# Expert slots of two widths in a routed transformer block: 64 of 256 rows and 7 of 128, written out

## What is computed

```
x = x + attention_block(layernorm(x))        # linear attention, 16 heads, MLP of 1024
xf = layernorm(x)
logits = xf @ gate_w.T                       # 8 experts
the 2 largest per token, softmax over the 2  # comb[token, expert]
out = sum over e of comb[:, e] * ((silu(xf @ wg[e].T) * (xf @ wu[e].T)) @ w_down[e].T)
shared = silu(xf @ sg_gate.T) * (xf @ sg_up.T) @ sg_down.T
x = x + shared + out
```

## Time and profile before

| | |
|---|---|
| median of 3 runs | 1746.89 us (1745.64 to 1747.42) |
| profiled execution, its own time | 1744.85 us |
| its span, first to last instruction | 1742.7 us (2.15 us lie around it) |
| PE / DVE / POOL / ACT busy | 96% / 67% / 67% / 52% of the span |
| mean granted clock of PE | 0.985 |
| first phase / expert phase | to about 1142 us / from there on |

### The profile page before, as it was taken

The page is one execution under the profiler, slowest core; times in us unless marked ns, Lnnn a source line. Parts: engine busy times, 40 slices in busy tenths (PEclk is TensorE's granted clock), DMA queues, the critical chain, the costliest instruction groups (busy, mean ns, idle before and its releaser), DMA issues.

```text
span 1742.7 us, 25628 instructions
## 1 busy us (share of the span) xinstructions
PE 1680.7 (96%) x7243; PEld 1227.5 (70%) x7289; DVE 1166.9 (67%) x1968; ACT 904.1 (52%) x2240; POOL 1166.9 (67%) x624
## 2 busy tenths in 40 slices
PE   6899999999999999999999998989999999999997
PEld 4555666666666666666666665578888888888886
DVE  7989999999999999999999993322222222222221
ACT  4356667667667667667667646522322322332322
POOL 5769889889889889889889881413333343343343
PEclk9898999999999999999999999999999999999999
DMA  4302211211211211111111111367777777777764
GB/s 151 116 13 61 62 49 37 62 49 36 61 49 36 61 49 36 59 50 36 54 55 37 37 49 37 92 169 162 165 154 160 165 157 156 167 158 156 168 158 78
DMA packets 89455, 157.20 MB, mean 90 GB/s; under 512 B 8896, under 2 KB 72128, under 8 KB 89024
## 3 DMA queue, kind: packets, MB, share of 16 engines
q1 hardware_dynamic: 60512, 112.58, 20.9%
q0 software_dynamic: 28896, 44.06, 14.9%
HBM read 101.79 MB, written 48.56 MB: 86 GB/s over the span
## 4 chain that ended last, share of the span: by engine, by line
PE 89%; ACT 5%; DVE 2%; issue 2%; DMA 1%; POOL 1%; SPq 1%; POOLq 0%; ACTq 0%; DVEq 0%
PE p_b L1494 17%; PE p_b L1548 13%; PE p_b L1698 10%; PE p_b L1709 10%; PE p_b L1641 8%; PE p_q L1698 7%; PE p_q L1466 6%; PE p_v L1698 4%; PE p_v L1466 3%; PE p_b L1480 2%; PE p_xT L1685 2%; PE p_xT L1626 2%; ACT rows L706 1%; ACT xmid L706 1%; PE p_b L1588 1%
## 5 line engine op out<-in xcount | busy, mean ns | idle before, releaser
L654 POOL DMA_INDIRECT out_rows<-prod_pool,prod x142 | 221.4, 1559 | 387.9 <-ACT prod_pool L949 357.5
L523 POOL TENSOR_TENSOR prod_pool<-prod_pool 128x2048 f32<-128x2048 f32 (+1 forms) x180 | 347.9, 1933 | 14.1
L1548 PE MATMUL p_b<-bT,fc_sb 128*128 128x512 f32 x512 | 231.5, 606 | 1.3 <-ACT bT L865 1.3
L1494 PE MATMUL p_b<-proj_sb,hid 128*128 128x256 f32 x1024 | 230.5, 379 | 0.0
L1494 PEld LDWEIGHTS p_b<-proj_sb,hid 128*128 128x128 f32 x1024 | 189.6, 190 | 29.4 <-issue 0.5
L1026 DVE TENSOR_TENSOR prod<-p_q,eqk 128x4096 f32<-128x4096 f32 (+1 forms) x47 | 184.0, 3914 | 5.3 <-DVE attn L1076 1.0
L1698 PE MATMUL p_b<-prod,exp_up 128*128 128x256 f32 x840 | 187.1, 379 | 0.0
L1063 DVE TENSOR_REDUCE qkv<-prod 128x256 f32<-128x4096 f32 (+1 forms) x47 | 183.7, 3910 | 1.6
L1050 DVE TENSOR_TENSOR prod<-p_q,v_dve 128x2048 f32<-128x2048 f32 (+2 forms) x60 | 177.4, 2956 | 1.5
L574 POOL DMA_INDIRECT rows_sorted<-rows,slot x128 | 125.7, 982 | 78.5 <-issue 34.5
L1035 DVE TENSOR_REDUCE p_q<-prod 128x128 f32<-128x2048 f32 (+2 forms) x60 | 177.4, 2957 | 1.1
(11 more groups left out here) (208 smaller groups left out, 2988.6 us busy)
## 6 DMA issues: line engine op xcount, KB each, us to landing
exp_up<-in_experts SPq DMA_DIRECT2D x71, 768.0 KB
prod<-rows_sorted SPq DMA_DIRECT2D x71, 260.0 KB
xin<-in_x SPq DMA_DIRECT2D x16, 512.0 KB, 3.4
xres<-in_x SPq DMA_DIRECT2D x16, 512.0 KB
xres<-xmid POOLq DMA_DIRECT2D x16, 512.0 KB, 4.6
out_rows<-x SPq DMA_DIRECT2D x16, 512.0 KB, 2.9
exp_dn<-in_experts SPq DMA_DIRECT2D x8, 384.0 KB, 5.8
out_rows<-prod_pool,prod POOLq DMA_INDIRECT x142, 3.8
```

Source lines behind the costliest of these rows:

```text
L523: done(g.tensor_tensor(prod_pool[:, at:at + n * w], prod_pool[:, at:at + n * w], prod_pool[:, at + n * w:at + 2 * n * w], ALU.add))
L654: pool.indirect_dma_start(out=out[:, :], out_offset=bass.IndirectOffsetOnAxis(ap=tok_i[j][:, a:a + 1], axis=0), in_=yg[j][:, a * D:(a + 1) ...
L1494: ins = t_.matmul(o, src[:, k, t * P:(t + 1) * P], w[:, k, :], start=k == 0, stop=bias_at is None and k == chunks - 1)
L1548: ins = t_.matmul(bnk[:], fc_sb[:, k, f * P:(f + 1) * P], bT[:, k, :], start=k == 0, stop=k == KC - 1)
```

## The change

The 71 slots become 64 of 256 rows and 7 of 128. The small ones are slots 9, 19, ... 69 (`halves`). The tables now have 72 places: 64 for wide slots and 8 for small ones (slot k reads place `in_table(k)`); an expert's rows are counted in pieces of 128, two pieces make a wide slot, and an odd piece goes to a small slot or to a wide slot left over. For a small slot each step does half the work: one load of 128 rows, two transposes, matmuls of 128 columns in `gate_up`, one half in `down`, in `weigh` and in `add`; the weights loaded are the same. `tables` gets more instructions, and POOL prepares more constants for it. Only one spare tile of empty rows is kept in DRAM, where there were eight.

The loops of the expert phase are gone: all 71 slots are written out on all five engines, so that places in the tables and the values waited for are constants. With this `tab_wait` falls away: a first-half add now always waits for both halves of the slot before.

```diff
-SORTED_TILES = 2 * TOKENS // TILE + EXPERTS - 1
-SPARE_TILES = EXPERTS
+WIDE = 2 * TOKENS // TILE
+SLOTS = WIDE + EXPERTS - 1
+TABLE = WIDE + EXPERTS
+SPARE_TILES = 1
...
+        def halves(k):
+
+            return 1 if k % 10 == 9 else SUB
+
+        def in_table(k):
+
+            return WIDE + k // 10 if k % 10 == 9 else k - k // 10
+
+        def rows_of_slots(n):
+
+            return SUB * n - n // 10
+
+        def adds(h, n):
+
+            return 16 * (n if h == 0 else n - n // 10)
...
                 if isinstance(c, int) and c == BLOCKS:
-                    g.iota(iota_k, [[1, SORTED_TILES]], base=0, channel_multiplier=0,
+                    g.iota(slot_i, [[1, TABLE]], base=-WIDE, channel_multiplier=0,
                            allow_small_or_imprecise_dtypes=True).then_inc(pool_const, 1)
-                    g.iota(iota_w, [[16, SORTED_TILES + 1]], base=0, channel_multiplier=0,
-                           allow_small_or_imprecise_dtypes=True).then_inc(pool_const, 1)
+                    done.later(g.iota(slot_q[:, 0:WIDE], [[1, WIDE]], base=0, channel_multiplier=0,
+                                      allow_small_or_imprecise_dtypes=True))
+                    done(g.memset(slot_half, 0.0))
+                    for i in range(EXPERTS // 2):
+                        at = WIDE + 2 * i
+                        done.later(g.memset(slot_q[:, at:at + 2], float(WIDE + i)))
+                        done.later(g.memset(slot_half[:, at + 1:at + 2], float(P)))
+                    done.sync()
+                    pool.sem_inc(pool_const, 1)
...
             def add(k, j):
 
-                if isinstance(k, int):
-                    before = 16 * k
-                else:
-                    before = pool.value_load(tab_wait[0:1, bass.ds(k, 1)], min_val=16, max_val=16 * SORTED_TILES)
-                for a in range(SUB):
-                    pool.wait_ge(y_ready, SUB * k + a + 1)
-                    wait(pool, added[a], 16 * k)
+                for a in range(halves(k)):
+                    pool.wait_ge(y_ready, rows_of_slots(k) + a + 1)
+                    wait(pool, added[a], adds(a, k))
                     if a == 0:
-                        wait(pool, added[1], before)
+                        wait(pool, added[1], adds(1, k))
                     stand_alone(pool)
                     pool.indirect_dma_start(
                         out=out[:, :], out_offset=bass.IndirectOffsetOnAxis(ap=tok_i[j][:, a:a + 1], axis=0),
                         in_=yg[j][:, a * D:(a + 1) * D], in_offset=None, compute_op=ALU.add
                         ).then_inc(added[a], 16)
...
+            for k in range(SLOTS):
+                add(k, k % 2)
...
             def tables():
 
                 announce(dve, v.tensor_scalar(pad_at[:], free_row[:], iota_p[:, 0:1], None, ALU.add), pads_at, 1)
...
+                pairs, singles = parts_of[:, 0, :], parts_of[:, 1, :]
+                done(v.tensor_tensor(subs_f, free_row[:], iota_r[:], ALU.subtract))
+                done(v.tensor_scalar(cnt_i, subs_f, float(P - 1), None, ALU.add))
+                done(v.tensor_scalar(cnt_i, cnt_i, P.bit_length() - 1, None, ALU.arith_shift_right))
+                done(v.tensor_copy(subs_f, cnt_i))
+                done(v.tensor_scalar(cnt_i, cnt_i, 1, None, ALU.arith_shift_right))
+                done(v.tensor_copy(pairs, cnt_i))
+                done(v.scalar_tensor_tensor(singles, pairs, -2.0, subs_f, ALU.mult, ALU.add))
+                done(v.tensor_copy(parts_to, parts_of))
                 for e in range(1, EXPERTS):
-                    done(v.tensor_tensor(tiles_to[:, e:e + 1], tiles_to[:, e:e + 1], tiles_to[:, e - 1:e], ALU.add))
-                over = prod[:, 0:SORTED_TILES * EXPERTS].rearrange("p (k e) -> p k e", e=EXPERTS)
-                wide = [P, SORTED_TILES, EXPERTS]
+                    done(v.tensor_tensor(parts_to[:, :, e:e + 1], parts_to[:, :, e:e + 1], parts_to[:, :, e - 1:e],
+                                         ALU.add))
+                over, one = (prod[:, lo:lo + TABLE * EXPERTS].rearrange("p (k e) -> p k e", e=EXPERTS)
+                             for lo in (0, TABLE * EXPERTS))
+                wide = [P, TABLE, EXPERTS]
+
+                def by_slot(z):
+                    return z.unsqueeze(2).to_broadcast(wide)
+
+                def by_expert(z):
+                    return z.unsqueeze(1).to_broadcast(wide)
+
+                def choose_from(at, yes, no):
+                    done(v.tensor_tensor(at, yes, no, ALU.subtract))
+                    done(v.tensor_tensor(at, at, is_wide, ALU.mult))
+                    done(v.tensor_tensor(at, at, no, ALU.add))
+                done(v.tensor_scalar(lacking, parts_to[:, 0, EXPERTS - 1:], -1.0, None, ALU.mult))
+                done(v.tensor_scalar(lacking, lacking, float(WIDE), None, ALU.add))
+                done(v.tensor_scalar(shift, lacking, 0.0, None, ALU.min))
+                done(v.tensor_tensor(shift, shift, lacking, ALU.add))
                 dve.wait_ge(pool_const, 8)
-                done(v.tensor_tensor(over, iota_k.unsqueeze(2).to_broadcast(wide),
-                                     tiles_to.unsqueeze(1).to_broadcast(wide), ALU.is_ge))
-                done(v.tensor_reduce(tab_e, over, AX.X, ALU.add))
+                done(v.tensor_scalar(slot_i, slot_i, shift[:, 0:1], None, ALU.add))
+                done.later(v.tensor_tensor(over, by_slot(slot_q), by_expert(parts_to[:, 0, :]), ALU.is_ge))
+                done(v.tensor_tensor(one, by_slot(slot_i), by_expert(parts_to[:, 1, :]), ALU.is_ge))
+                done.later(v.tensor_reduce(e_wide, over, AX.X, ALU.add))
+                done(v.tensor_reduce(e_one, one, AX.X, ALU.add))
+                done.later(v.tensor_tensor(over, over, by_expert(pairs), ALU.mult))
+                done(v.tensor_tensor(one, by_expert(iota_e[:]), by_slot(e_one), ALU.is_equal))
+                done.later(v.tensor_reduce(first_of, over, AX.X, ALU.add))
+                done(v.tensor_tensor(one, one, by_expert(pairs), ALU.mult))
+                done.later(v.tensor_reduce(one_of, one, AX.X, ALU.add))
+                done(v.tensor_scalar(is_wide, e_wide, float(EXPERTS), None, ALU.is_lt))
+                choose_from(tab_e, e_wide, e_one)
                 done(v.tensor_scalar(tab_ei, tab_e, float(EXPERTS - 1), None, ALU.min))
...
+                done(v.tensor_tensor(first_of, slot_q, first_of, ALU.subtract))
+                done(v.scalar_tensor_tensor(first_of, first_of, float(TILE), slot_half, ALU.mult, ALU.add))
+                done(v.tensor_scalar(one_of, one_of, float(TILE), None, ALU.mult))
+                choose_from(slot_q, first_of, one_of)
+                v.scalar_tensor_tensor(tab_row, tab_e, float(REGION), slot_q, ALU.mult, ALU.add
                                        ).then_inc(tables_ready, 1)
...
+            for k in range(SLOTS):
+                tile(k, k % 2)
...
             def gT(k, j):
-                pe.wait_ge(xg_loaded[j], 16 * (k // 2 + 1) if isinstance(k, int) else 8 * (k - j) + 16)
+                pe.wait_ge(xg_loaded[j], 16 * (k // 2 + 1))
                 wait(pe, gT_ready, k)
                 for c in range(KC):
-                    for h in range(SUB):
-                        ins = t_.transpose(p_xT[:, (c * SUB + h) * P:(c * SUB + h + 1) * P],
+                    for h in range(halves(k)):
+                        at = c * halves(k) + h
+                        ins = t_.transpose(p_xT[:, at * P:(at + 1) * P],
                                            xg[j][:, h, c * P:(c + 1) * P], ident[:])
                 ins.then_inc(gT_psum, 1)
 
             def gate_up(k, j):
 
-                pe.wait_ge(up_loaded[j], 16 * (k // 2 + 1) if isinstance(k, int) else 8 * (k - j) + 16)
+                pe.wait_ge(up_loaded[j], 16 * (k // 2 + 1))
                 pe.wait_ge(gT_ready, k + 1)
                 wait(pe, hg_ready, HCH * (k - 1))
                 for i in range(HCH):
                     for part in range(2):
                         for c in range(KC):
                             at = c * 2 * HALF + part * HALF + i * P
-                            ins = t_.matmul(gu_banks[j][i][:, part * TILE:(part + 1) * TILE],
-                                            exp_up[j][:, at:at + P], xgT[j][:, c * TILE:(c + 1) * TILE],
+                            n = halves(k) * P
+                            ins = t_.matmul(gu_banks[j][i][:, part * n:(part + 1) * n],
+                                            exp_up[j][:, at:at + P], xgT[j][:, c * n:(c + 1) * n],
                                             start=c == 0, stop=c == KC - 1)
                     ins.then_inc(gu_psum, 1)
 
             def down(k, j, e):
                 pe.wait_ge(hg_ready, HCH * (k + 1))
-                wait(pe, y_ready, SUB * k)
-                for h in range(SUB):
+                wait(pe, y_ready, rows_of_slots(k))
+                for h in range(halves(k)):
                     for i in range(HCH):
```

(70 more changed lines are left out.)

57 lines of the change are left out of this document (20 added, 37 removed).

## The result

| | before | changed |
|---|---|---|
| median | 1747.16 us (1745.64 to 1748.04, 4 runs) | 1799.49 us (1776.25 to 1804.84, 4 runs) |
| ratio | | 1.0267, 95% interval 1.0185 to 1.0348 |
| profiled execution | 1744.85 us, span 1742.7 | 1776.25 us, span 1774.5 |

The forecast was 1715.0 us (range 1710 to 1728); the kernel became slower, by 1.9 to 3.5%. Six runs are on record, from 1776.25 to 1807.87 us (the median is of four of them); the ratio is taken over the four that lie within 1.5% of the fastest, without 1804.84 and 1807.87. The profile is of the fastest run, so it shows less of the loss than the median has.

A forecast was written before the change was run, and what follows sets the result against it. PE was taken to bound the expert phase at 8.21 us a slot. -28.7 - 1.3 - 1.9 = -31.9 us took the profiled 1744.85 us to 1713.0, and 2.04 more gave the median, 1715.0 (range 1710 to 1728).

The forecast's parts named there:

- Small slots, -28.7: Expert phase: each of seven small slots saves PE 4.10 us, with gate and up at 0.108 us an instruction.
- Between the phases, -1.3: Longer `tables` delays the first phase's last down, but PE's clock may recover sooner: -1.3 us, ends -3.3 and +1.5.
- low for half of it: Between the phases: clock low for half of the down, which ends at 1143.6; gate and up 0 ends 2.1 us sooner.
- Weight loads in time: Expert phase: weights land within 5.8 us of the shortest 8.4 us available behind a small slot, so no cost.
- Code fetch at nothing: Written-out expert phase: about 20 packets fetched, costed at nothing; slower through code fetch was a rival at about 1760, chance 0.06.
- The adds ... Nothing: Expert phase: first-half adds wait about 0.1 us before a small slot; what hangs on them has some us in hand.
- waits for DMA or for an add: Rival, expert phase: a small slot waits for DMA or an add, two us each, giving 1729; chance 0.04.
- The tail, -1.9: Kernel end: slot 69's second-half add is gone and its first is issued 1.86 us sooner: -1.9 us, bounds 0 and 3.1.

The follow-up runs named there:

- e7_four_deep_own_half: Changed kernel with four buffers, not two, for row weights and token numbers, and the table of waits back: 1715.34 us, ratio 0.9833 to the kernel before.
- e6_one_small: Changed kernel with only slot 9 small and the other 70 wide: 1826.14 us, ratio 1.0469 to the kernel before.
- e4_no_weight_loads: Changed kernel without weight loads from slot 2 on, reusing the weights of slots 0 and 1: 1713.34 us, ratio 0.9818 to the kernel before.

## Why the prediction was wrong, point by point

**Small slots, -28.7: right.** Gate and up of slot 9 run from 1217.85 to the down at 1220.53: 2.68 us for 24, 0.112 each (0.108 taken). A small slot saves 4.0 us, seven 28.1. `e7_four_deep_own_half` has it in the whole time: 1745.77 to 1715.34 are 30.4 us, and 28.1, the 1.55 and the 0.8 of the next points make 30.45. Load and stream of 128 columns lie beside each other; in series they would be 0.214. Here the rule of the Trainium skill (TensorE: Matmul & The Clock Gate, section The mechanism) that a load overlaps only where it goes to other rows of the array is contradicted at 128 columns too; the same section also names loads into a background weight buffer, which would allow it.

**Between the phases, -1.3: right.** The timeline there (the counterpart of the earlier trace rows): `tables` ends at 1132.5 (forecast 1132.4), the down starts at 1135.59 (1135.8), and the first gate and up runs at full speed:

```profile
1132.30 0.23 DVE L1420 SCALAR_TENSOR_TENSOR prod<-prod,prod_pool 128x72 int32<-128x72 f32 x1
...
1134.16 1.49 SPq L483 DMA_DIRECT2D exp_up<-in_experts  x2
...
1135.59 8.43 PE L1521 MATMUL p_b<-sgdn_sb,sg_g 128*128 128x256 f32 x24 [3.84 <-DVE sg_g L1427]
...
1145.29 3.69 PE L1727 MATMUL p_q<-prod,exp_up 128*128 128x256 f32 x16 [0.84 <-ACT prod L947]
```

The windows of 1 us (as the earlier trace rows) show the low level, 1.2 GHz, behind PE's idle time of 3.84 us, and its end inside the down, the case "low for half of it":

```profile
1136.00:1137.00 1.00, 1.00 (x3) 0.76 (x3) 0.00 (x0) 0.00 (x0) 0.00 (x0) 0.50 0.77 209
...
1141.00:1142.00 1.00, 1.00 (x5) 0.82 (x4) 0.00 (x0) 0.00 (x0) 0.00 (x0) 0.67 1.00 323
```

The down ends at 1143.9 (1143.6 in that case), and the transposes behind gate and up 0 start at 1150.55 where they started at 1152.10: 1.55 us sooner, 1.3 forecast. That the two are so close is partly luck: the case that came true gave 2.1 by itself, and 1.3 was taken between the cases.

**Weight loads in time: right.** The runs with four buffers have them at full PE. (The shortest time is 8.65 us and not 8.4, since both transposes counted are of wide slots: a little more in hand, not less.)

**Code fetch at nothing: right**, some 20 packets forecast, 23 fetched in that queue and 21 in a second one; that they cost nothing is shown by the wide slots written out. (A small slot has 64 PE records, not 41, since its 24 of gate and up stay; the 20 packets hardly change by that.)

**"The adds ... Nothing": this step failed.** It put the adds at nothing, with 3.8 us of landing from the earlier trace rows, where weights were issued 3.9 us ahead of the first-half add and 2.4 behind the second, and used it for an add beside which weights start. I worked out for the weights whether they come in time for PE, but not what they meet on the way; the first such add, the second half of slot 7, took 7.5 us, and 6.6 is the median behind it. And I let the wait end there ("some us in hand"): the row weights hold `keep_meta`, that the row load, that the next weights. I had both waits in the text, DVE's queue too, but not SP's queue behind them, which closes the ring. What came in place of nothing: in the profiled run PE idles 44.5 us for 1.3, 42.8 of it waiting for rows. The rival "waits for DMA or for an add" had the place, at 2 us a small slot; it lacked that the loss goes on in wide slots, about 1.4 us in each (`e6_one_small`).

**The tail, -1.9: too much by 1.1.** In the changed kernel the adds are late already. In `e7_four_deep_own_half` the spans end 10.1 us behind PE's last instruction (1702.43 and 1712.5), in the kernel before 10.9 (1731.84 and 1742.7): 0.8 us. The second half of slot 69 is gone, as forecast, and the last first half waits for that slot's only half instead, 3.05 us beside 3.09 in the earlier trace rows. But that only half doesn't come as early against PE as the first half of slot 69 did. In the kernel before, ACT released it, 2.56 us ahead of PE's end:

```profile
1729.28 1.56 POOL L654 DMA_INDIRECT out_rows<-prod_pool,prod  x1 [4.34 <-ACT prod_pool L949]
```

In `e7_four_deep_own_half` it waits for the add before it to land, and comes 1.41 us ahead:

```profile
1701.02 1.56 POOL L674 DMA_INDIRECT out_rows<-prod_pool,prod  x1 [3.04 <-DMA out_rows<-prod_pool,prod]
1705.62 1.56 POOL L674 DMA_INDIRECT out_rows<-prod_pool,prod  x1 [3.05 <-DMA out_rows<-prod_pool,prod]
```

The difference, 1.15 us, is what was missing.

**Open.** What ends the state at some small slots and not at others, and with it the spread of the runs (1776 to 1808 us), wasn't isolated. That SP's order is part of the ring rests on the timeline; the run meant to test it didn't.

## What to carry to other kernels

When a change shortens one step of a steady rotation, list the transfers that its end triggers and look what they will start beside, at the new time: a landing time read from the steady state holds only for its spacing. Then follow each wait that gets longer through every queue to the place where it started; a ring of waits longer than the bottleneck's turn turns one disturbance into a lasting loss. A deeper buffer at one link of the ring (here a few columns of row weights) may be all it needs.

## What the runs showed of the hardware

An indirect add of 128 rows lands late where a 768 KB load of weights is issued near it. In the changed kernel, from 1160 to 1740 us, pairing each add with the nearest such load:

| nearest load of weights | adds | us to landing: least, median, most |
|---|---|---|
| 3.3 us or more ahead of the add | 26 | 3.7, 3.8, 4.9 |
| 0.5 to 3.3 us ahead | 1 | 5.6 |
| within 0.5 us | 33 | 4.9, 6.9, 9.0 |
| 0.5 to 1.7 us behind it | 28 | 3.9, 6.4, 7.3 |
| 1.7 to 2.2 us behind it | 9 | 3.7, 3.9, 4.5 |
| 2.2 us or more behind it | 29 | 3.6, 3.8, 4.6 |

So an add whose load comes 2.2 us later is as quick as the adds without any loads beside them (3.8 us in `e4_no_weight_loads`), and 1.5 us isn't enough. With four buffers, where the spacing differs from slot to slot, the median within 0.5 us is 5.5 (20 adds).
